# Score products in both halves of the partitions, two passes issued together, and the bias in 64-row products

## The chip, the core and the metric

The kernel runs on one core of a Trainium2 chip. The metric is the device time of one execution in microseconds. The core has five engines that run side by side: TensorE (PE, with its weight loads shown as PEld), VectorE (DVE), ScalarE (ACT), GpSimd (POOL) and SyncE (SP), which here only issues DMAs and waits. Engines meet through semaphores: an instruction waits until a count is reached, and adds to a count when it is done. Each engine takes its own instructions in order.

## What is computed

One transformer layer on 4 sequences of 1024 tokens with 128 channels: a layer norm, attention with 16 heads of 8 channels and relative positions, and a mixture of 64 experts with a shared one. Attention is what the change touches. With `rp` the distance key - query, clipped to -31..31:

```
q, k, v = heads of xn @ w_qkv.T          # q scaled by 8 ** -0.5
attn = q k^T
     + (q @ rpe_k_table)[.., rp]         # by query and distance
     + (k * scale @ rpe_q_table)[.., rp] # by key and distance
attn = softmax(attn)
out  = attn v + (sums of attn by distance) @ rpe_v_table
x    = x + out @ w_proj.T + b_proj + experts(xn) + shared(xn)
```

There are 4 x 16 = 64 pairs of sequence and head, called heads below. Scores of one head are 1024 x 1024.

## The kernel before

**Score rows.** Float32 factors are cut into bfloat16 parts. One score tile has 32 keys (partitions of the output) and up to 512 queries (columns), and is one product whose contraction runs over rows 0 to 72 or 0 to 78 of `Ks` (keys) and `Qs` (queries): 48 rows of six combinations of parts of q and k (`q_stack`, `k_stack`), three rows for the negated row maximum (`ROW_M`, filled by `Qs<-mparts`), and rows for the constant bias of far distances (`q_far`, `k_far`; 6 more rows for the keys above the window). Four such tiles, one for each 32 partitions of the output, fill a bank of PSUM: this is a *unit* of 128 keys `J` and one half of the queries. A head has 16 units. Near the diagonal (96 columns for each 32 keys) the bias depends on the exact distance; it is added by products with `eye3` (a stack of three 32 x 32 identities) as weights and a window `WT` of three parts (96 rows) as the moving side.

**Two passes.** Pass 1 makes the scores of a head; DVE takes maxima out of PSUM (L1408, one instruction a unit). Then DVE forms the row maximum, PE turns it (L914), DVE cuts it in three parts (`mparts`, L1421 to L1425) and SP writes them to the three rows `ROW_M` of `Qs` (L488). Pass 2 makes the same scores again, now less the maximum, and ACT takes their exponentials to `PT` (L1096). PE multiplies them with the values (`values`, products `PS<-PT,Vst`) and sums them by distance (`near`, products `PS<-WP,TOE`).

**The order of the work** is written out by hand. Every engine runs `iteration(i, c, peeled)` for head `h`, on PE, DVE and ACT in 16 slots `s`. In slot `s`, PE makes unit `s` of pass 1 of head `h + 1` and unit `s - 6` of pass 2 of head `h` (in slots 0 to 5 the last units of head `h - 1`). Each pass has two banks of PSUM of its own, so a unit waits until the one before last has been read (`s1_read` by DVE, `s2_read` by ACT).

**The window's round trip.** The near bias is prepared ahead, and goes through memory twice to be shifted by distance. In slot 11 PE makes the query part of head `h + 4` (L918, `PS<-Qs,tab`); ACT copies it to `dq_e` (L1115); SP writes it to `dq_d` (L544) and reads it back sheared as `dq_s` (L483). In slot 5 of the next iteration PE transposes `dq_s` and adds the key part (L944 and `PS<-tab,Ks`); ACT, DVE and POOL cut it in parts `ajp`; SP writes these to `aj_d` (L524) and reads them, sheared again, as the windows `WT` (L498).

**SP's queue.** In each iteration SP goes through one list in order: `TOE` (every second head), `dq_s` (waits until `dq_d` has landed), the three maximum rows (wait for `mparts`), four loads for the queries of head `h + 4` (`load_queries`), three windows of head `h + 2` (L498), three loads of keys of head `h + 4` (`load_keys`), `aj_d` of head `h + 3` (waits for POOL), `dq_d` of head `h + 4` (waits for ACT's copy). Some iterations have others between: `acc_d` and `xn_d` in the first eleven, weights of experts in iterations 13, 16, 22 and 24.

The 16 steps of the experts' products run alone after head 29, between 762 us and 846 us of the trace, and the loop over heads then goes on.

**Padding.** Lines 975 to 977 add instructions on PE that do nothing else than raise `paced`, so that each head has 1024 instructions on PE (`BLOCK`, `PER_HEAD`).

## Time and profile before

| | |
|---|---|
| median of 3 runs | 1529.62 us (1525.92 to 1534.31) |
| span of the profiled execution, first to last instruction | 1522.0 us |
| busy: PE, DVE, ACT, POOL | 87%, 73%, 52%, 36% of the span |
| score products (`PS<-Qs,Ks`) | 11904, 666.4 us busy |
| bias products (`PS<-WT,eye`) | 4352, 294.7 us busy |
| maxima by DVE (L1408) | 1024, 689.7 us busy, 699 ns each |
| packets moved by SP's DMA queue | 155414, 52.5% of the 16 DMA engines' span |
| mean granted clock of TensorE | 0.937 |

The page gives no time for the profiled execution apart from its span; the span is 7.6 us under the median of the runs. Busy times of PE are those of overlapping instructions whose ends are modelled: four products in four column groups run at once, so PE's busy share says little about how much of it is taken. DMA-issuing instructions are not counted as busy on any engine; they are seen in the timeline as SPq.

### The profile page before, as it was taken

To read this page: it belongs to the slowest core of one execution; us is meant where nothing else is said; L and a number is where in the kernel's file an instruction comes from. 1 tells how busy PE (TensorE), PEld (TensorE's weight loads), DVE (VectorE), ACT (ScalarE), POOL (GpSimd) and SP (SyncE) were. 2 spreads that over 40 slices of the span, in tenths; PEclk is the share of its full clock that TensorE was granted. 3 is DMA by queue.
4 is the path that set the end of the run, shared out by engine and by line. 5 is a ranking of instruction groups with operands and counts; after the bars stand their busy time and mean duration, and the time that the engine had idled before them with its cause. 6 is when DMAs were issued, how large, how long until landed. Compare 5 with 4: busy or idle time off the path is not lost. (4 is left out here: it accounts for less than half of the span.)

```text
span 1522.0 us, 75140 instructions
## 1 busy us (share of the span) xinstructions
PE 1325.6 (87%) x32698; PEld 895.9 (59%) x32698; DVE 1111.2 (73%) x2461; ACT 797.9 (52%) x1408; POOL 541.3 (36%) x552
## 2 busy tenths in 40 slices
PE   2785399999999999988989899999999999999887
PEld 1352256666666666655668565666666666666555
DVE  7684378888888888887764676777777767777762
ACT  1332135655665666655541455665666555656544
POOL 3453212222222222222434244444444444444423
PEclk9897559999999999999995799999999999999999
DMA  4444546666556555554564566666666666666532
GB/s 97 138 142 138 159 158 200 200 207 193 186 183 191 190 176 183 181 184 153 174 189 145 160 183 182 183 192 198 186 183 196 183 176 180 190 183 183 149 104 58
DMA packets 167209, 260.10 MB, mean 171 GB/s; under 512 B 33980, under 2 KB 89397, under 8 KB 166886
## 3 DMA queue, kind: packets, MB, share of 16 engines
q1 hardware_dynamic: 155414, 248.46, 52.5%
q0 software_dynamic: 11472, 6.83, 3.7%
q8 instruction: 264, 4.33, 1.1%
q14 instruction: 59, 0.48, 0.1%
HBM read 145.14 MB, written 112.37 MB: 169 GB/s over the span
## 5 line engine op out<-in xcount | busy, mean ns | idle before, releaser
L1408 DVE TRANSPOSE_TENSOR_REDUCE tops<-PS 128x16 f32<-128x512 f32 x1024 | 689.7, 699 | 190.1 <-PE PS L697 183.9
L1096 ACT ACTIVATE PT<-PS 128x512 f32<-128x512 f32 x1024 | 590.2, 596 | 423.4 <-PE PS L697 416.1
L697 PE MATMUL PS<-Qs,Ks 73*32 73x512 bf16 (+29 forms) x11904 | 666.4, 322 | 66.8 <-DVE tops L1408 45.6
L697 PEld LDWEIGHTS PS<-Qs,Ks 73*32 73x32 bf16 (+1 forms) x11904 | 308.9, 97 | 266.7 <-DVE tops L1408 94.0
L697 PE MATMUL PS<-PT,Vst 128*9 128x256 f32 (+7 forms) x7552 | 345.4, 286 | 12.6 <-issue 12.1
L638 POOL COPY WP<-PT 128x768 f32<-128x768 f32 x128 | 105.3, 822 | 645.4 <-ACT PT L1096 460.9
L697 PE MATMUL PS<-WT,eye 96*32 96x96 bf16 (+2 forms) x4352 | 294.7, 206 | 0.2 <-issue 0.2
L697 PEld LDWEIGHTS PS<-PT,Vst 128*9 128x9 f32 x7552 | 187.8, 91 | 82.6 <-issue 32.3
L697 PEld LDWEIGHTS PS<-WT,eye 96*32 96x32 bf16 x4352 | 186.8, 99 | 22.5 <-issue 1.2
L657 POOL TENSOR_TENSOR ajp<-dq_s,ajp 128x508 bf16<-128x508 f32 x128 | 147.3, 1151 | 10.4
L626 POOL DMA_INDIRECT acc_d<-XNA,tok_i x64 | 100.8, 1575 | 78.8 <-DMA acc_d<-XNA,tok_i 66.2
L1120 ACT ACTIVATE ajp<-PS 128x508 bf16<-128x508 f32 x128 | 76.8, 600 | 95.4 <-PE PS L697 95.4
L655 POOL CAST ajp<-dq_s 128x508 bf16<-128x508 f32 x128 | 78.7, 615 | 125.2 <-DVE dq_s L1449 125.2
L944 PE MATMUL PS<-ident,dq_s 127*128 127x127 f32 x512 | 86.5, 295 | 39.5 <-DMA dq_s<-dq_d 39.3
L697 PE MATMUL PS<-WP,TOE 128*32 128x32 f32 x6144 | 110.1, 197 | 5.4 <-issue 4.7
L697 PEld LDWEIGHTS PS<-WP,TOE 128*32 128x32 f32 x6144 | 103.8, 111 | 18.3 <-issue 17.4
L1449 DVE TENSOR_TENSOR dq_s<-PS,ajp 128x508 f32<-128x508 f32 x128 | 83.2, 650 | 27.9 <-ACT ajp L1120 27.9
L1115 ACT ACTIVATE dq_e<-PS 128x1024 f32<-128x1024 f32 x64 | 65.6, 1024 | 41.7 <-PE PS L697 41.7
L944 PEld LDWEIGHTS PS<-ident,dq_s 127*128 127x128 f32 x512 | 58.4, 151 | 46.9 <-issue 44.2
L1454 DVE TENSOR_TENSOR Ym<-PS,ymask 128x256 f32<-128x256 f32 x64 | 27.2, 425 | 75.6 <-PE PS L697 75.6
L697 PE MATMUL PS<-PT,WT 128*88 128x512 f32 (+2 forms) x128 | 56.0, 632 | 18.5 <-DVE Ym L1290 6.2
L697 PE MATMUL PS<-tab,Ks 79*128 79x127 bf16 x512 | 53.6, 231 | 0.0
(199 smaller groups left out, 1025.9 us busy)
## 6 DMA issues: line engine op xcount, KB each, us to landing
aj_d<-ajp SPq DMA_DIRECT2D x64, 768.0 KB
WT<-aj_d SPq DMA_DIRECT2D x192, 256.0 KB
dq_d<-dq_e SPq DMA_DIRECT2D x64, 512.0 KB, 5.3
dq_s<-dq_d SPq DMA_DIRECT2D x64, 512.0 KB, 3.9
TOE<-toe_d SPq DMA_DIRECT2D x33, 768.0 KB, 5.8
q_stack<-PT SPq DMA_DIRECT2D x24, 256.0 KB, 2.5
Qs<-q_stack SPq DMA_DIRECT2D x64, 96.0 KB
Ks<-k_stack SPq DMA_DIRECT2D x64, 96.0 KB
```

What stands on the lines that cost most here:

```text
L626: pool.indirect_dma_start(out=acc_d, out_offset=bass.IndirectOffsetOnAxis(ap=tok_i[:, 1 + half, n:n + 1], axis=0), in_=Y[:, n, :], in_offs ...
L638: pool.tensor_copy(WP[:, 4 * part:4 * part + 4, :], src).then_inc(win_in[part], 1)
L655: pool.tensor_copy(low[:, 0], r1).then_inc(aj_mid, 1)
L657: pool.tensor_tensor(low[:, 1], r1, low[:, 0], ALU.subtract).then_inc(aj_parts, 1)
L697: return pe.matmul(o, l, r, start=start, stop=stop, skip_group_check=True)
L944: pe.matmul(PS[:, bank, a * P:a * P + DIST], dq_s[0:DIST, J * P:(J + 1) * P], ident[0:DIST, 0:DIST], start=a == 0, stop=False, is_transpos ...
L1096: act.activation(PT[:, TILE + N * J + 512 * half:TILE + N * J + 512 * half + 512], PS[:, 2 + u % 2, :], ACT.Exp).then_inc(s2_read, 1)
L1115: act.activation(dq_e[:, :], MISC, ACT.Copy).then_inc(dq_copied, 1)
L1120: act.activation(ajp[:, 0, 4 * part:4 * part + 4, 0:DIST], PS[:, 6 + part, :].rearrange("p (a n) -> p a n", n=P)[:, :, 0:DIST], ACT.Copy). ...
L1408: dve.tensor_reduce(tops[:, (h + 1) % 2, s // 2, 16 * (s % 2):16 * (s % 2) + 16], PS[:, s % 2, :].rearrange("p (c i) -> p c i", i=TILE), A ...
L1449: dve.tensor_tensor(dst, src, ajp[:, 0, 4 * part:4 * part + 4, 0:DIST], ALU.subtract).then_inc(aj_copied, 1)
L1454: dve.tensor_tensor(Ym[:, :].rearrange("p (t a x) -> p a t x", t=NJ, x=4), PS[:, 6, 0:256].rearrange("p (a t x) -> p a t x", t=NJ, x=4), y ...
```

## The change

1. `Qs`, `Ks` and `tab` get 128 partitions. The 48 + 15 = 63 rows of the contraction (`ROW_M` moves from 64 to 48) lie in partitions 0 to 62 and again in 64 to 126. Queries are written to both halves. Keys are written once: even key tiles `J` to the upper half, odd ones to the lower. `tab` has three planes, the last one for odd tiles in the lower half.
2. A score product of tile `J` takes its rows from half `J % 2`, so it uses 64 rows. Pass 1's unit and pass 2's unit of one slot have key tiles three apart, so they are in different halves.
3. The new `units` waits for everything that either unit needs, and then issues their products in turn: the first pieces of both, the second pieces of both, the bias of both; the two counts `s1_ready` and `s2_ready` are raised at the end.
4. The bias of a window is two 64-row products: `eye3` over the first two parts, and `eye64` over the third part, which lies in planes 4 and 5 of `WT`, 32 rows for each pair of `s`.
5. DMAs follow: maxima six times instead of three, queries nine instead of four, windows eight instead of three (shorter runs of 512 instead of 1024 elements), keys six instead of three.
6. Keys are projected in the column order that suits this; `near` goes round the four column groups evenly; the padding of PE's instructions (L975 to L977) is dropped; DVE makes `eye64` once.

The diff, cut to its core:

```diff
-ROW_M = 64
-ROW_L = 73
-ROW_K = 73
-ROWS = 79
+ROW_M = 48
+ROW_L = 57
+ROW_K = 57
+ROWS = 63
+HALF = 64
...
-        QUERIES = 16 * 4
-        KEYS = 16 * 3
+        QUERIES = 16 * 9
+        KEYS = 16 * 6
+        WINDOWS = 16 * 8
+        MAXIMA = 16 * 6
...
             def load_queries(h):
-                sp.dma_start(Qs[0:48, r, :], q_stack[...]).then_inc(stack_in[r], 16)
-                sp.dma_start(tab[0:48, r, :, :], tab_stack[...]).then_inc(stack_in[r], 16)
-                sp.dma_start(Qs[ROW_M:ROW_M + 3, r, :], zero_d).then_inc(stack_in[r], 16)
-                sp.dma_start(Qs[ROW_M + 6:ROW_M + 12, r, :], q_far[hh, :, tok]).then_inc(stack_in[r], 16)
+                for side in range(2):
+                    top_row = HALF * side
+                    sp.dma_start(Qs[top_row:top_row + 48, r, :], q_stack[...]).then_inc(stack_in[r], 16)
+                    sp.dma_start(Qs[top_row + ROW_M:top_row + ROW_M + 3, r, :], zero_d).then_inc(stack_in[r], 16)
+                    sp.dma_start(Qs[top_row + ROW_M + 6:top_row + ROW_M + 12, r, :], q_far[hh, :, tok]).then_inc(stack_in[r], 16)
+                for v, row, m in ((0, 0, 0), (1, 0, 1), (1, HALF, 2)):
+                    sp.dma_start(tab[row:row + 48, r, m, :], tab_stack[...]).then_inc(stack_in[r], 16)
...
+            def load_windows(t):
+                for side in range(2):
+                    for row, planes, part, s in ((0, (0, 4), 0, 0), (TILE, (0, 4), 1, 0), (0, (4, 6), 2, 0), (TILE, (4, 6), 2, 2)):
+                        row += HALF * side
+                        sp.dma_start(WTb[row:row + TILE, t % 3, planes[0]:planes[1], :, :].rearrange("p s j n -> p s (j n)"),
+                                     shear(t % 2, part, side, s, planes[1] - planes[0])).then_inc(wt_in[t % 3], 16)
...
-                    for n in range(3):
-                        sp.dma_start(Qs[ROW_M + n:ROW_M + n + 1, ...], mparts[:, n, :]).then_inc(mrow_in, 16)
+                    for side in range(2):
+                        for n in range(3):
+                            row = HALF * side + ROW_M + n
+                            sp.dma_start(Qs[row:row + 1, ...], mparts[:, n, :]).then_inc(mrow_in, 16)
...
+            def scores(h, bank, J, half, n):
+                ins, row, r = None, HALF * (J % 2), h % RING
+                for s, k, w in pieces(J, half)[n]:
+                    key = P * (J // 2) + TILE * s
+                    ins = mm(PS[TILE * s:TILE * s + TILE, bank, w[0] - 512 * half:w[1] - 512 * half],
+                             Ks[row:row + k, r, key:key + TILE], Qs[row:row + k, r, w[0]:w[1]], start=n == 0)
+                return ins
+
+            def bias(h, bank, J, half, low):
+                ins, row = None, HALF * (J % 2)
+                for s, w, a in near_columns(J, half):
+                    eye = eye64[row:row + HALF, TILE * (s // 2):TILE * (s // 2) + TILE] if low else eye3[row:row + HALF, :]
+                    ins = mm(PS[TILE * s:TILE * s + TILE, bank, w[0] - 512 * half:w[1] - 512 * half], eye,
+                             WTb[row:row + HALF, h % 3, 4 + s % 2 if low else s, J // 2, a:a + w[1] - w[0]], start=False)
+                return ins
+
+            def units(first, second):
+                if first is not None:
...
+                    wait(pe, s1_read, SLOTS * h + u - 1)
+                if second is not None:
+                    h, u = second
+                    if u == 0:
+                        pe.wait_ge(mrow_in, MAXIMA * (h + 1))
+                    wait(pe, s2_read, SLOTS * h + u - 1)
...
+                for n in range(2):
+                    for k, *unit in both:
+                        last[k] = scores(*unit, n) or last.get(k)
+                for low in range(2):
+                    for k, *unit in both:
+                        last[k] = bias(*unit, low) or last[k]
...
-                    if on(1):
-                        unit(i, c + 1, s, 0)
+                    behind = (h, s - LAG) if s >= LAG else (h - 1, s + SLOTS - LAG)
+                    units((h + 1, s) if on(1) else None, behind if 0 <= behind[0] < HEADS else None)
...
-                    if s >= 12 and h >= 0:
-                        spare = BLOCK - PER_HEAD - (EXTRA if j_r == 2 else EXTRA + 1 if h == LISTS else 0)
-                        pause(spare // 4 + (s - 12 < spare % 4))
```

**How instructions move.** The first place is SP's list in a middle iteration, from the maximum rows to the last load for the queries. Before:

```order
L488 DMA Qs<-mparts 1x32x32 [waits mparts_ready]
L488 DMA Qs<-mparts 1x32x32 x2
L452 DMA Qs<-q_stack 48x1024 [waits s2_ready]
L453 DMA tab<-tab_stack 48x256
L455 DMA Qs<-zero_d 3x1024
L456 DMA Qs<-q_far 6x1024
```

The same place in the changed kernel:

```order
L506 DMA Qs<-mparts 1x32x32 [waits mparts_ready]
L506 DMA Qs<-mparts 1x32x32 x5
L454 DMA Qs<-q_stack 48x1024 [waits s2_ready]
L456 DMA Qs<-zero_d 3x1024
L457 DMA Qs<-q_far 6x1024
L454 DMA Qs<-q_stack 48x1024
L456 DMA Qs<-zero_d 3x1024
L457 DMA Qs<-q_far 6x1024
L459 DMA tab<-tab_stack 48x128 x3
```

Seven DMAs have become 15, with the same waits at the same two of them.

The second place is the rest of SP's list, from the windows to `dq_d`. Before:

```order
L498 DMA WT<-aj_d 32x4x1024 [waits s2_ready,aj_out]
L498 DMA WT<-aj_d 32x4x1024 x2
L461 DMA Ks<-k_stack 48x1024
L463 DMA Ks<-k_far 3x1024 x2
L524 DMA aj_d<-ajp 128x3x1024 [waits wt_in0,aj_parts]
L544 DMA dq_d<-dq_e 128x1024 [waits dq_in,dq_copied]
```

And in the changed kernel:

```order
L485 DMA WT<-aj_d 32x4x512 [waits s2_ready,aj_out]
L485 DMA WT<-aj_d 32x4x512
L485 DMA WT<-aj_d 32x2x512 x2
L485 DMA WT<-aj_d 32x4x512 x2
L485 DMA WT<-aj_d 32x2x512 x2
L468 DMA Ks<-k_stack 48x2x256
L471 DMA Ks<-k_far 3x2x256 x2
L468 DMA Ks<-k_stack 48x2x256
L471 DMA Ks<-k_far 3x2x256 x2
L540 DMA aj_d<-ajp 128x3x1024 [waits wt_in0,aj_parts]
L560 DMA dq_d<-dq_e 128x1024 [waits dq_in,dq_copied]
```

Six DMAs have become 14 before `aj_d`, which with `dq_d` stays at the end of the list.

The third place is PE's stream in slot 6, where pass 2 of a head begins (`Qs,Ks` are score products, `WT,eye` bias products; "32x512" is 32 keys by 512 queries). Before:

```order
L697 MATMUL PS<-Qs,Ks 32x352 [waits s1_read]
L697 MATMUL PS<-Qs,Ks 32x384
L697 MATMUL PS<-Qs,Ks 32x416
L697 MATMUL PS<-Qs,Ks 32x448
L697 MATMUL PS<-Qs,Ks 32x160
L697 MATMUL PS<-Qs,Ks 32x128
L697 MATMUL PS<-Qs,Ks 32x96
L697 MATMUL PS<-Qs,Ks 32x64
L697 MATMUL PS<-WT,eye 32x96 x3
L697 MATMUL PS<-WT,eye 32x64
L697 MATMUL PS<-Qs,Ks 32x512 [waits s2_read,mrow_in]
```

In the changed kernel:

```order
L713 MATMUL PS<-Qs,Ks 32x352 [waits s2_read,mrow_in,s1_read]
L713 MATMUL PS<-Qs,Ks 32x384
L713 MATMUL PS<-Qs,Ks 32x416
L713 MATMUL PS<-Qs,Ks 32x448
L713 MATMUL PS<-Qs,Ks 32x512 x2
L713 MATMUL PS<-Qs,Ks 32x32
L713 MATMUL PS<-Qs,Ks 32x64
L713 MATMUL PS<-Qs,Ks 32x160
L713 MATMUL PS<-Qs,Ks 32x128
L713 MATMUL PS<-Qs,Ks 32x96
L713 MATMUL PS<-Qs,Ks 32x64
```

The wait for the maximum rows (`mrow_in`) stood behind pass 1's unit 6 and now stands ahead of it, and the products of the two units alternate.

## Rows read from the trace of the kernel before

**Rows 1.** Two stretches: length, busy PE, PEld, DVE, ACT, POOL, clock, DMA share, GB/s
```profile
420.00:690.00 270.00, 246.27 (x6960) 166.41 (x6958) 230.69 (x521) 161.43 (x286) 71.63 (x84) 1.00 0.59 184
862.00:1440.00 578.00, 538.52 (x15125) 369.28 (x15121) 427.67 (x880) 344.92 (x605) 252.44 (x245) 0.99 0.65 184
```
**Rows 2.** L1404 on DVE, once a head, 190:780 and 840:1490: count, durations, first and last start
```profile
L1404 DVE TENSOR_REDUCE top<-tops x30: 587/597/623, 198.4 to 762.6; 128x32 f32<-128x256 f32 x30
L1404 DVE TENSOR_REDUCE top<-tops x34: 580/612/622, 846.6 to 1480.6; 128x32 f32<-128x256 f32 x34
```
**Rows 3.** Chain that ended last, 862:1440, shares by line
```profile
by line: PE PS L697 47.3%; DMA dq_d<-dq_e 12.6%; DMA dq_s<-dq_d 9.7%; DVE tops L1408 8.5%; PE PS L944 5.5%; issue 4.7%; ACT dq_e L1115 3.4%; DVE dq_s L1449 3.0%; PE PS L932 2.0%; ACT PT L1096 1.9%; PE PS L914 0.5%; DVE mparts L1421 0.2%; DV
```
**Rows 4.** SP's timeline, one iteration: start, us from first issue to last end, count
```profile
546.80 0.33 SPq L483 DMA_DIRECT2D dq_s<-dq_d  x1
549.92 1.78 SPq L488 DMA_DIRECT2D Qs<-mparts  x3
551.88 0.44 SPq L452 DMA_DIRECT2D Qs<-q_stack  x1
552.36 0.42 SPq L453 DMA_DIRECT2D tab<-tab_stack  x1
552.83 0.30 SPq L455 DMA_DIRECT2D Qs<-zero_d  x1
553.17 0.27 SPq L456 DMA_DIRECT2D Qs<-q_far  x1
553.54 1.86 SPq L498 DMA_DIRECT2D WT<-aj_d  x3
555.45 0.43 SPq L461 DMA_DIRECT2D Ks<-k_stack  x1
555.92 0.61 SPq L463 DMA_DIRECT2D Ks<-k_far  x2
559.32 0.39 SPq L524 DMA_DIRECT2D aj_d<-ajp  x1
560.22 1.34 SPq L544 DMA_DIRECT2D dq_d<-dq_e  x1
...
565.03 0.32 SPq L483 DMA_DIRECT2D dq_s<-dq_d  x1
```
**Rows 5.** SP's waits, 862:1440: us in total, times, longest
```profile
SPq L524 <- POOL ajp L657: 87.0, 31, 6.8
SPq L488 <- DVE mparts L1425: 63.4, 30, 4.7
```
**Rows 6.** DMA issues: dq_d 420:690 and 862:1440, maxima 420:690, median us to landing
```profile
dq_d<-dq_e SPq DMA_DIRECT2D x14, 512.0 KB, 4.8
dq_d<-dq_e SPq DMA_DIRECT2D x30, 512.0 KB, 5.7
Qs<-mparts SPq DMA_DIRECT2D x42, 2.0 KB, 1.7
```
**Rows 7.** L544 (dq_d), 862:1440: landing, shortest, median, longest
```profile
DMA to landing us min/median/max: 4.9/5.7/6.8
```
**Rows 8.** Issues of windows (420:690) and maxima (862:1440): ns min/median/max
```profile
L498 SPq DMA_DIRECT2D WT<-aj_d x42: 320/428/1412, 420.4 to 670.9; - x42
L488 SPq DMA_DIRECT2D Qs<-mparts x90: 518/588/1713, 873.8 to 1428.4; - x90
```
**Rows 9.** PE's timeline near slot 5: start, us, count
```profile
550.84 0.94 PE L697 MATMUL PS<-Qs,Ks 79*32 79x512 bf16 x16
551.61 0.21 PE L697 MATMUL PS<-WT,eye 96*32 96x96 bf16 x4
551.76 0.65 PE L944 MATMUL PS<-ident,dq_s 127*128 127x127 f32 x4
```
**Rows 10.** DVE's last cut of the maxima, and ACT's first exponential of that head
```profile
549.72 0.17 DVE L1425 CAST mparts<-mx 32x32 bf16<-32x32 f32 x1
554.44 1.08 ACT L1096 ACTIVATE PT<-PS 128x512 f32<-128x512 f32 x2 [0.19 <-PE PS L697]
```

More of the change, by code:

```diff
@@ L496, in iteration @@
                     wait(sp, s2_ready, SLOTS * h)
[L497 to L499 removed]
+                    load_windows(t)
                 if on(4):
@@ L813, in scores @@
-                return bias(bank, half, J, r3) or ins
-            def unit(i, c, u, which):
-                h, r = c, c % RING
-                ready, read, bank = ((s1_ready, s1_read, 0), (s2_ready, s2_read, 2))[which]
-                if which == 0 and u == 0:
-                    pe.wait_ge(stack_in[r], QUERIES * (h // RING + 1))
-                    pe.wait_ge(keys_in[r], KEYS * (h // RING + 1))
-                    pe.wait_ge(wt_in[h % 3], 48 * (h // 3 + 1))
-                if which == 1 and u == 0:
-                    pe.wait_ge(mrow_in, 48 * (h + 1))
-                wait(pe, read, SLOTS * h + u - 1)
-                J, half = u // 2, u % 2
-                scores(bank + u % 2, half, J, r, h % 3).then_inc(ready, 1)
+                            own[n].append((s, ROWS if kind == "U" else ROW_L, w))
@@ new lines, in pieces, with near_columns @@
+                            n += 1
+                return own
+            def near_columns(J, half):
+                own = []
+                for s in range(4):
+                    t = 4 * J + s
+                    w = span(max(TILE * (t - 1), 0), min(TILE * (t + 2), N), half)
+                    if w:
+                        own.append((s, w, w[0] - TILE * (t - 1)))
+                return own
+            def scores(h, bank, J, half, n):
[5 more added lines that the diff above has]
+                return ins
```

117 lines of the change are left out of this document (52 added, 65 removed).

## The prediction, written before the changed kernel ran

> **What bounds the kernel now.** I read first which stretches repeat: L1404 runs once a head, and its starts give the period, (762.6 - 198.4) / 29 = 19.46 us a head before the experts' stretch and (1480.6 - 846.6) / 33 = 19.21 us after it [rows 2]. These 62 periods are 1198 of the 1522 us, and the change touches little else. Then the busy times: DVE, which has no overlap inside it, is busy 230.69 / 270 x 19.46 = 16.6 us a head in the first stretch (where it also routes tokens) and 427.67 / 578 x 19.21 = 14.2 us in the second [rows 1]. So no engine but PE can be full, and PE's busy time is of overlapping products. Third the chain: in the second stretch 22.3% of it are the transfers of `dq_d` and `dq_s`, most of the rest is PE [rows 3]. That is the round trip, ACT's copy, `dq_d`, `dq_s`, PE's slot 5, then six slots of PE, and again: the two transfers are 0.223 x 19.21 = 4.3 us a head on average over heads that hang on them and heads that don't.
>
> Last, and it decides here, SP's own timeline [rows 4]. One iteration takes 18.23 us from one `dq_s` to the next (546.80 to 565.03). SP goes idle in it three times: 3.1 us for the maxima, 2.8 us for POOL's `ajp` (556.53 to 559.32), and for the landing of `dq_d`, issued at 560.22, 4.81 us before the next `dq_s`. The rest is issuing, back to back: each DMA holds SP for 0.27 to 0.6 us plus some 0.05 us to the next.
>
> **SP's cycle without its two idle waits.** From the starts in [rows 4]: `dq_s` 0.37 (with its gap), three maxima 1.83, `q_stack` 0.48, `tab` 0.47, `zero_d` 0.34, `q_far` 0.37, three windows 1.91, `k_stack` 0.47, two `k_far` 0.66, `aj_d` about 0.45, and `dq_d` to the next `dq_s` 4.81. Sum 12.2 us, so in 18.2 us SP has 6.0 us of slack. In the second stretch the waits for POOL and for the maxima are (87.0 + 63.4) / 31 = 4.9 us a head [rows 5]; that is what SP can give there before it sets the pace.
>
> **The changed list, part by part**, at the same price for the same kind of DMA [rows 4]; whether a half-sized DMA costs SP less is bounded below.
> - Maxima: six at 0.61 = 3.66 us (was 1.83).
> - Queries: (0.48 + 0.34 + 0.34) twice and `tab` three times 0.47 = 3.73 us (was 1.66).
> - Windows: eight. Three took 1.91 us in this iteration with one of them held up; the median is 0.428 [rows 8], 0.47 with its gap, so eight are 3.76 us, and 4.4 us with one held up by 0.6 (1.91 less three times 0.47 is 0.5, and the longest issue of all is 1.41).
> - Keys: twice 0.47 and four times 0.33 = 2.26 us (was 1.13).
> - `dq_s` 0.37, `aj_d` 0.45, `dq_d` until landing and next `dq_s` 4.81.
>
> Sum 3.66 + 3.73 + 4.4 + 2.26 + 0.37 + 0.45 + 4.81 = 19.7 us. This is a loop by itself: `dq_s` waits for `dq_d` of the iteration before, and `dq_d` stands at the end of the list. Nothing that PE gains shortens it. SP's waits for `mparts`, `s2_ready`, `aj_parts` and `dq_copied` should be over when it arrives: `aj_d` now comes some 14 us after `dq_s`, where POOL's parts were ready after 12.5 us (546.80 to 559.32).
>
> First stretch: 19.7, and weights of experts (8 DMAs), `acc_d` and `xn_d` (about 22) stand in the same list, some 20 us in all by 0.43 to 1 us each (an estimate from `k_stack` at 0.43 and `dq_d` at 1.34), 0.7 us a head: 20.4 us against 19.46, +0.9 x 29 = +27 us. Second stretch: `dq_d` lands after 5.7 instead of 4.8 us [rows 6], and one maximum in four is held up (median 0.588, longest 1.713) [rows 8], say 0.5 us a head: 19.7 + 0.9 + 0.5 = 21.1 us against 19.21, +1.9 x 33 = +63 us.
>
> **What is hidden.** PE: 16 products of three units take 0.77 us to the next (550.84 to 551.61), 0.26 a unit, 32 units 8.2 us a head; if two halves run side by side that is 4.1 us less. Bias: four products cost at most 0.15 us (551.61 to 551.76) [rows 9], and the 4352 of them are 17 such groups a head, which double: at most +2.6 us, below it near zero where they fall beside the other half. Both lie under SP's cycle. Dropped padding: nothing in the trace shows it as cost or gain; I take 0, within -0.2 and +0.5 us a head, as PE has slack now. Shorter `WT` runs, 768 instead of 384 packets, and 96 KB more for queries: the DMA engines are 59 and 65% busy [rows 1], 11.5 and 12.5 us of a period; twice the queries is +96 KB on about 3.6 MB moved in a head, and more packets than bytes at most +15%, 1.8 us on engines with 7 us to spare. It can lengthen `dq_d`'s landing, which is in the range. Start: memsets, `eye64` and six maxima for the first head, +2 us, inside the rounding.
>
> A place where the chip's notes speak: the Trainium skill, "DMA: Bandwidth & Descriptors", Rules for kernel authors, says that two transfers to disjoint partition halves are no gain since they serialize on the same engines, and to use one of 128 partitions. Here both halves are loaded apart, with the same bytes twice. The trace bears it out on the issuing side, where every DMA holds SP whatever its size (0.30 us for `zero_d`, 6 KB, and 0.44 for `q_stack`, 96 KB) [rows 4]. By that rule too the sum goes up; it changes no term.
>
> Sum: 1522.0 + 27 + 63 = 1612 us of span, + 7.6 by which the median stands over the span: I predict **1620 us**.
>
> **Bounds.** Low: nothing held up and each DMA at its median (19.0 us), landing 4.9 at best in the second stretch [rows 7], other DMAs 10 us in all. That is 19.4 and 19.1 us a head, -5 us in all: 1525. Half-sized windows at the shortest issue seen (0.320) [rows 8] take another 0.9 us: 1470. High: landing 6.8 [rows 7] and every group held up once more: 21.3 and 22.8 us a head, +53 and +119: 1702.
>
> **Rivals.**
> 1. *SP's issues overlap or shrink and the engines gain.* If the 16 more DMAs held SP less than 6.0 us in the first and 4.9 us in the second stretch, that is 0.3 to 0.37 us each, SP stays off the path. Then the round trip binds, with six slots of PE in it, 12 units, of which half go: -1.5 us a head; DVE's 16.6 allows that. 62 x -1.5 = -93: 1437 us. For it: the engines' waits name PE everywhere. Against it: only `zero_d`, `q_far` and `k_far` are near 0.3 [rows 4]. Chance 0.16.
> 2. *The maxima land late and PE holds pass 1 behind them.* From DVE's last cut (549.72 + 0.17) to the first exponential are 4.55 us [rows 10]; issues take 1.78 and landing 1.7 after the last issue begins [rows 4, 6], so about 1 us is spare. Six issues take 1.83 more: the exponential comes 0.8 to 1 us later, and since pass 1's unit 6 now waits too, DVE runs out. Where SP's cycle is not longer, the period is 19.3 + 0.9 less what PE gains elsewhere, 0 to 1 us: 19.2 to 20.2, that is 1525 to 1585 us. It would be told from mine by PE's wait for `Qs<-mparts` with SP idle. Chance 0.08.
> 3. *The halves don't run side by side.* PE then keeps its 8.2 us, gets 2.6 us of bias, and loses more at changes of shape. It had little slack, so 19.3 + 2.6 and more: 22 to 23 us, +200 us: 1730. Chance 0.05. The Trainium skill, "TensorEngine Tiling (Array Packing)", Key Properties, says that a change of tiling mode drains TensorE. Values keep 128 rows and alternate with the 64-row units, so by the rule there are some 16 drains more a head. At a change of that kind now (551.61 to 551.76, from 32-column tiles to a whole-array transpose) the row leaves at most 0.15 us for products and drain together [rows 9], 2.4 us a head, which SP's cycle covers unless this rival holds.
>
> **How the numbers follow.** Mine 0.68, the rivals 0.16, 0.08 and 0.05, 0.03 for what I haven't thought of. About 0.5% (8 us) either way is what a measurement can tell from none. Of my 0.68, bounds leave 0.03 within that and 0.03 below. Rival 1 is faster, rival 2 slower by two thirds, rival 3 slower. So faster 0.19, same 0.06, slower 0.75. The range leaves rivals 1 and 3 out and takes in mine: 1505 to 1700.
>
> **What would show it.** The starts of L1404 20 to 21 us apart. SP's timeline without idle time between `dq_s` and `aj_d`: about 13.5 us of issues end to end, and its waits for POOL's `ajp` and `mparts` near zero; only the wait for `dq_d` stays. PE's waits for `dq_s<-dq_d` in slot 5 up from few to nearly every head, and DVE's and ACT's idle time up with them. Two units together in 0.3 us or less if the halves run side by side. I am wrong if SP still idles 2 us or more for POOL or `mparts`, or if one of its DMAs takes clearly under 0.3 us.

## The result, and the profile after

The changed kernel takes 1830.83 us (median of 4 runs, 1815.33 to 1837.52) against 1527.77 us of the kernel before on the same chip: ratio 1.199, 95% interval 1.1915 to 1.2064. The prediction had the direction and missed the size: 1620 was forecast, with a range up to 1700.

Some executions of a kernel took longer at a lower granted clock, and differences, ratios and the table below leave them out: without them the medians of `b_mrow6`, `b_rest`, `b_shift`, `a_mrow3` and `a_shift` are 1778, 1608, 1691, 1760 and 1846 us, where the medians of all their runs are 1794, 1614, 1715, 1764 and 1849, and the profile of `b_shift` is of such an execution, at 1742.

The page of the changed kernel: span, busy PE and granted clock in 40 slices, queues, and the groups that answer to [rows 1, 5, 9].

```profile
span 1831.2 us, 84602 instructions
PE 1302.5 (71%) x36988; PEld 852.9 (47%) x37050; DVE 1111.4 (61%) x2462; ACT 796.6 (43%) x1408; POOL 540.8 (30%) x552
PE   3782776767667777777779677777776777777677
...
PEclk9895689898888888889875888888888889999888
...
q1 hardware_dynamic: 219542, 257.17, 45.1%
...
q8 instruction: 297, 4.87, 1.1%
...
PE 19%; SPq 8%; issue 7%; DMA 6%; DVE 6%; ACT 0%
...
L713 PE MATMUL PS<-Qs,Ks 57*32 57x512 bf16 (+29 forms) x11904 | 460.4, 347 | 235.4 <-issue 117.8
...
L713 PE MATMUL PS<-WT,eye 64*32 64x96 bf16 (+2 forms) x8704 | 288.8, 212 | 45.1 <-issue 45.0
```

Nobody became busier, everybody waits more. Score products are busy 460.4 us where they were 666.4, yet PE sat idle 235.4 us in front of them (66.8 before), half of it behind "issue", which means that nothing the profile shows held it. The clock's slices are 8 where nearly all were 9. SP's queue, 0% of the chain on the page of before, has 8% of it.

The two stretches (columns as in [rows 1]), the once-a-head DVE instruction as in [rows 2], and the chain of 1100:1700:

```profile
500.00:900.00 400.00, 291.38 (x9133) 188.50 (x9135) 266.05 (x606) 186.28 (x328) 87.20 (x102) 0.86 0.47 147
1100.00:1700.00 600.00, 435.19 (x14213) 287.65 (x14238) 358.92 (x738) 287.81 (x506) 206.72 (x200) 0.90 0.53 154
```
```profile
L1433 DVE TENSOR_REDUCE top<-tops x29: 582/599/636, 199.8 to 887.2; 128x32 f32<-128x256 f32 x29
...
L1433 DVE TENSOR_REDUCE top<-tops x31: 580/598/616, 1071.2 to 1786.2; 128x32 f32<-128x256 f32 x31
```
```profile
by line: PE PS L713 31.6%; issue 15.5%; DMA dq_d<-dq_e 8.4%; DVE tops L1437 7.1%; SPq L485 6.4%; DMA dq_s<-dq_d 5.8%; SPq L506 5.0%; PE PS L976 4.0%; DVE dq_s L1478 2.9%; SPq L459 2.3%; SPq L468 2.0%; SPq L471 1.8%; SPq L454 1.2%; PE PS L96
```

The period is (887.2 - 199.8) / 28 = 24.55 us a head, then (1786.2 - 1071.2) / 30 = 23.8 us, where it was 19.46 and 19.21 [rows 2]; 62 periods of some 4.8 us more are the 300 us. In the chain "issue" has 15.5%, 3.7 us a head, three times its share in [rows 3].

SP's timeline, the iteration that answers to [rows 4]; then its waits and PE's in 1100:1600 (total, times, longest), as in [rows 5]:

```profile
612.28 0.32 SPq L499 DMA_DIRECT2D dq_s<-dq_d  x1
613.60 3.79 SPq L506 DMA_DIRECT2D Qs<-mparts  x6
617.44 0.58 SPq L454 DMA_DIRECT2D Qs<-q_stack  x1
...
619.71 1.23 SPq L459 DMA_DIRECT2D tab<-tab_stack  x3
621.04 3.68 SPq L485 DMA_DIRECT2D WT<-aj_d  x8
...
627.85 0.39 SPq L540 DMA_DIRECT2D aj_d<-ajp  x1
628.34 0.43 SPq L560 DMA_DIRECT2D dq_d<-dq_e  x1
633.25 0.33 SPq L499 DMA_DIRECT2D dq_s<-dq_d  x1
640.50 0.52 SPq L506 DMA_DIRECT2D Qs<-mparts  x1
```
```profile
SPq L499 <- DMA dq_d<-dq_e: 90.8, 21, 7.6
SPq L506 <- DVE mparts L1454: 41.6, 17, 6.9
```
```profile
PE PS L713 <- issue: 89.7, 67, 4.8
PE PS L713 <- DVE tops L1437: 29.1, 43, 0.8
PE PS L976 <- DMA dq_s<-dq_d: 10.0, 7, 2.4
```

The issue costs came out as priced: six maxima 3.79 us, eight windows 3.68. POOL's `ajp` is no longer waited for. But after its next `dq_s` SP waits 6.9 us for the maxima (633.58 to 640.50): it is not SP alone that sets the pace, PE is late too: it stood still 89.7 us of 500 with "issue" as the reason, 4.8 us at the longest. The first stretch lost more than the second: its periods are 4.15 us over the 20.4 forecast, the second's 2.7 us over 21.1.

### The profile page after: what moved, and what is told of

The parts are those of the page before. It is cut to its first block and busy times, and to the rows that moved or that the text cites. A ratio compares the mean times of both kernels' runs of the same rounds, so it can differ in the third digit from the quotient of the medians.

```text
span 1831.2 us, 84602 instructions
## 1 busy us (share of the span) xinstructions
PE 1302.5 (71%) x36988; PEld 852.9 (47%) x37050; DVE 1111.4 (61%) x2462; ACT 796.6 (43%) x1408; POOL 540.8 (30%) x552
## 3 DMA queue, kind: packets, MB, share of 16 engines
q8 instruction: 297, 4.87, 1.1%
## 5 line engine op out<-in xcount | busy, mean ns | idle before, releaser
L713 PE MATMUL PS<-Qs,Ks 57*32 57x512 bf16 (+29 forms) x11904 | 460.4, 347 | 235.4 <-issue 117.8
L713 PE MATMUL PS<-PT,Vst 128*9 128x256 f32 (+7 forms) x7552 | 379.4, 312 | 56.4 <-issue 55.2
L713 PEld LDWEIGHTS PS<-Qs,Ks 57*32 57x32 bf16 (+1 forms) x11904 | 169.8, 93 | 434.9 <-issue 216.8
L713 PE MATMUL PS<-WT,eye 64*32 64x96 bf16 (+2 forms) x8704 | 288.8, 212 | 45.1 <-issue 45.0
L713 PEld LDWEIGHTS PS<-WT,eye 64*32 64x32 bf16 x8704 | 260.3, 102 | 87.9 <-issue 56.5
L713 PEld LDWEIGHTS PS<-PT,Vst 128*9 128x9 f32 x7552 | 171.6, 96 | 171.8 <-issue 85.2
L976 PE MATMUL PS<-ident,dq_s 127*128 127x127 f32 x512 | 108.5, 350 | 68.5 <-DMA dq_s<-dq_d 68.3
L673 POOL TENSOR_TENSOR ajp<-dq_s,ajp 128x508 bf16<-128x508 f32 x128 | 147.7, 1154 | 10.4
L713 PE MATMUL PS<-WP,TOE 128*32 128x32 f32 x6144 | 88.8, 199 | 19.1 <-issue 17.9
L713 PEld LDWEIGHTS PS<-WP,TOE 128*32 128x32 f32 x6144 | 79.3, 112 | 26.9 <-issue 22.2
L1143 ACT ACTIVATE dq_e<-PS 128x1024 f32<-128x1024 f32 x64 | 65.6, 1024 | 49.3 <-PE PS L713 49.3
L713 PE MATMUL PS<-tab,Ks 128*128 128x127 bf16 x512 | 65.3, 266 | 0.0
```

The lines of the kernel that those rows point to most:

```text
L673: pool.tensor_tensor(low[:, 1], r1, low[:, 0], ALU.subtract).then_inc(aj_parts, 1)
L713: return pe.matmul(o, l, r, start=start, stop=stop, skip_group_check=True)
L976: pe.matmul(PS[:, bank, a * P:a * P + DIST], dq_s[0:DIST, J * P:(J + 1) * P], ident[0:DIST, 0:DIST], start=a == 0, stop=False, is_transpos ...
L1143: act.activation(dq_e[:, :], MISC, ACT.Copy).then_inc(dq_copied, 1)
```

## What stops TensorE with nothing to wait for

I numbered PE's instructions in the trace and looked where it stopped without a semaphore. The stops stand at multiples of 256: in `b_shift`, 53 of 57 successive stops of 0.5 us and more lie a whole number of 256 instructions apart. The queue named instruction (q8) brings such blocks: 297 packets of 16 KB, 4.87 MB, for some 76200 instructions of PE in the changed kernel (297.6 times 256), and 264 packets for 67700 in the kernel before (264.6 times 256). An example from the run `b_shift` below, PE's timeline:

```profile
1038.93 0.37 PE L697 MATMUL PS<-PT,Vst 128*9 128x96 f32 x6
1040.73 0.60 PE L697 MATMUL PS<-PT,Vst 128*9 128x64 f32 x10 [1.42 <-issue]
```

PE stops in the middle of 16 value products. The packet with the next block ran from 1038.33 to 1039.28, and PE went on 1.44 us after its end; over all stops of 0.5 us and more at block ends in the changed kernel this lag is 1.28 to 1.52 us (10th to 90th percentile, median 1.39). The packet began only 1.0 us before PE was through (1039.30), so whether a block end costs anything depends on what PE does around it: where PE waits for another engine anyway, the block arrives unseen (0.06 us a block in `b_mrow6`, below).

The kernel before has 1024 instructions a head, four blocks, so its block ends stand at the same four places in every head, and the empty instructions are what keeps them there. The changed kernel has 1157 and no padding: 4.5 blocks, whose ends move through all places. This and two more quantities, worked out from the traces: stops over 0.3 us at block ends, their sum over the number of blocks in 420:690 and 862:1440; time at the lower clock, 1.2 GHz, for each period of the loop over heads, from 240 us on and without the experts' part; last maximum landed after DVE's last cut, median in 862:1440. In the slower kernels the experts' part lies later and so within 862:1440 (887 to 982 us in `b_mrow6`); without it the stops come out nearly the same.

```
kernel        median   instr.  stop per  low clock  maxima landed
               us      a head  block us  us a head   us
before        1524-39  1024     0.14        0.4       3.7
b_actq        1523     1024     0.15        0.4       3.5
b_nopad       1617     1007     0.41        2.6       3.8
b_rest        1608     1024     0.28        1.6       3.7
b_bias2       1631     1143     0.46        1.7       3.6
b_shift       1691     1024     0.53        6.1       3.0
b_mrow6       1778     1024     0.06        7.8       6.2
b_splist      1828     1024     0.14        8.8       6.3
a_both        1557     1024     0.51        1.6       3.0
h_wide_m3     1621     1024     0.47        1.3       3.0
a_thin        1699     1157     0.74        2.9       3.6
h_wide        1761     1024     0.36        5.0       5.8
h_wide_p64    1790     1024     0.46        5.7       5.5
h_wide_p192   1802     1024     0.60        4.8       5.4
a_mrow3       1760     1157     0.71        3.8       4.1
a_nolow       1776     1024     0.43        5.5       5.9
h_wide_p128   1894     1024     0.83        8.2       5.2
a_actq        1816     1157     0.81        5.5       5.7
after         1831     1157     0.90        5.7       5.8
a_shift       1846     1157     0.85        6.0       5.9
```

Kernels with one time only (`a_both`, `a_thin`, `a_nolow`, `b_splist`) had the kernel before at 1538 beside them; the others were run four to ten times, with the kernel before at 1524 to 1539. Where DMAs of a head are counted below, `dq_s` is left out: 15 before, 31 in the changed kernel.

## The experiments

**First round: SP's list or TensorE.** Theory A: SP's longer list and the stops at block ends, each a part. Theory B: the list is all. Theory C: the products' shapes.

`a_thin`: the changed kernel with SP's list cut to 15 DMAs a head; after the first round of buffers the loads for the odd tiles' half and the maxima for it are left out, so its output is another one.

```diff
-                for side in range(2):
+                for side in range(2 if h < RING else 1):        # queries, keys; maxima and windows alike
```

> The changed kernel, with the DMAs for the lower half of the partitions left out after the first round of buffers (so SP's list has 15 DMAs a head again, not 31; the scores of odd key tiles are computed from stale rows). Theory A (two causes: SP's list costs about 1 to 1.5 us a head over the old period, and PE's stalls at every 256th instruction, where the next block of instructions is fetched, cost the rest): SP's share goes, PE's stalls stay: 1620 to 1720 us, L1433 21 to 22.5 us apart, PE still stalled some 2 to 4 us a head at block boundaries. Theory B (SP's list is all of it; PE's stalls only fill time that SP leaves): 1440 to 1540 us.

Measured 1699.04 us, beside 1538 of the kernel before: some 140 us of the 300 are gone with the list, not all. B falls.

`a_nolow`: the changed kernel without the second of the two 64-row bias products, and with three empty instructions a head, 1024 in all (bias of every third window left out).

```diff
-                for low in range(2):
+                for low in range(1):
...
+                    if s == 12 and h >= 0:
+                        pause(3)
```

> The changed kernel without the products with eye64 (the third part of the near bias is left out), and 3 empty instructions a head on PE, so that a head has 1024 instructions on PE again (four blocks of 256) instead of 1157. SP's list stays at 31 DMAs. Theory A: stalls at block boundaries fall to under 1 us a head, the period becomes SP's cycle of about 20.5 us: 1600 to 1680 us. Theory B: SP's list is untouched, so at most the 2.6 us a head of bias products could go, and none of it is on SP's path: 1780 to 1840 us. Theory C (64-row products next to 128-row ones make PE wait at each change of shape): changes of shape are the same, so 1780 us or more.

Measured 1775.82 us. Only some 60 us, a miss: a whole number of blocks is not yet a good place for their ends, and the maxima still came late.

`a_both`, both edits together:

> Both edits at once: no eye64 products and 1024 instructions a head on PE, and SP's list of 15 DMAs. Theory A: neither cause is left, and what the halves side by side give is seen: 17.3 to 18.5 us a head, 1420 to 1500 us. Theory B: the same as with the thin list alone, within 1%. Theory C: over 1600 us, since the changes of shape are all there.

Measured 1556.73 us. So with a short list, three maxima, the third part of the bias left out and 1024 instructions, scores in both halves cost 19 us against 1538 and gain nothing at this place of the block ends. C, which wanted over 1600, falls; A had hoped for a gain that isn't there. Whether it would be there at another place was not tested: PE stopped 0.51 us a block here for 0.14, 1.5 us a head more.

`b_splist`: the kernel before, with the same bytes in the changed kernel's 31 DMAs a head (queries 9, keys 6, windows 8, maxima 6, each cut in smaller ones). Of its edit, the part on the maxima:

```diff
-                    for n in range(3):
-                        sp.dma_start(Qs[ROW_M + n:ROW_M + n + 1, h % RING, :]..., mparts[:, n, :])
+                    for n in range(3):
+                        for z in range(2):
+                            sp.dma_start(Qs[ROW_M + n:ROW_M + n + 1, h % RING, 512 * z:512 * z + 512]..., mparts[16 * z:16 * z + 16, n, :])
```

> The kernel before, with the same bytes in 31 DMAs a head on SP instead of 15 (each cut in two or three, the numbers by kind as in the changed kernel). PE's instructions and their padding are untouched. Theory A: SP's cycle of 20 to 21 us sets the period: 1590 to 1660 us, SP's waits for POOL's parts and for the maxima near zero, stalls of PE at block boundaries as before. Theory B: 1780 us or more.

Measured 1828.46 us, with the old products and hardly a stop at a block end. In this single run the list alone makes the old kernel as slow as the changed one: A's 1590 to 1660 is a miss. B had this right, and `a_thin` and `a_both` wrong. Something in the list costs far more than its length.

**Second round: which DMAs, and is it the number of instructions.** All on the kernel before.

`b_mrow6` has only the edit just shown (three DMAs more); `b_rest` all the others (13 more, maxima in three).

> The kernel before with only the row maxima copied in six DMAs of half the size in place of three, the count of the changed kernel. Theory M (what SP's longer list costs is mostly that the maxima land later and pass 1 waits behind them): 2.1 us a head more before they have landed, twice if the lower clock follows, so 1660 to 1800 us. Rival L (the whole list's length costs, by SP's cycle): 3 DMAs more of 16 that SP's slack of 5 to 6 us takes in: 1530 to 1560 us.

> The kernel before with every other DMA of a head cut as in the list with 31 DMAs (queries 9, keys 6, windows 8), the maxima left in three. Theory M: the maxima leave SP at once, so most of the 290 us that the full list cost are gone: 1560 to 1640 us. Rival L: 13 DMAs more, 5.5 us a head, nearly all of the list's price: 1740 to 1820 us.

Measured 1794.06 us and 1614.08 us (ratio 1.042, 1.036 to 1.048). Three DMAs of 0.6 us cost 240 us, thirteen others 70. Theory M holds. The waits of PE in `b_mrow6`, 862:1440, then what follows such a wait (columns as in [rows 1]):

```profile
PE PS L698 <- DMA Qs<-mparts: 42.1, 21, 2.5
...
PE PS L698 <- issue: 4.8, 7, 1.7
```
```profile
862.00:1440.00 578.00, 513.42 (x11391) 348.02 (x11381) 348.52 (x721) 266.38 (x476) 205.13 (x200) 0.82 0.54 153
```
```profile
1006.00:1018.00 12.00, 11.62 (x346) 8.45 (x340) 8.26 (x19) 6.41 (x13) 2.40 (x2) 0.96 0.47 143
1018.00:1020.40 2.40, 0.41 (x26) 0.25 (x14) 1.29 (x2) 0.53 (x2) 1.35 (x2) 1.00 0.07 6
1020.40:1024.40 4.00, 4.00 (x68) 2.48 (x69) 2.29 (x4) 1.81 (x4) 2.81 (x4) 0.57 0.67 171
1024.40:1028.20 3.80, 3.67 (x86) 1.98 (x86) 2.83 (x6) 2.62 (x5) 1.78 (x2) 1.00 1.07 305
```

PE waits 2.0 us in 21 of 22 heads. After the wait (0.41 us busy of 2.4) the granted clock falls to 0.57 on average for 4 us, that is nearly all at 1.2 GHz, and PE does 68 products in 4.0 us, 17 a us, where it did 346 in 12, 29 a us.

The mean clock of 0.82 can't be turned into a price for a head, because this stretch takes in the experts' part, and the clock is low there in the kernel before too (52 us, all else of its trace after 250 us 30). A stretch of that kind, then one behind a wait for the maxima, then the heads behind the experts' part:

```profile
914.80:1007.00 92.20, 87.09 (x779) 67.17 (x782) 42.16 (x106) 24.00 (x51) 28.91 (x29) 0.50 0.48 138
1303.90:1314.10 10.20, 10.20 (x203) 6.00 (x191) 4.74 (x9) 4.50 (x7) 3.34 (x3) 0.50 0.76 218
1007.00:1440.00 433.00, 380.57 (x9595) 251.57 (x9587) 276.26 (x556) 217.67 (x383) 160.56 (x154) 0.89 0.56 158
```

The price is seen when the periods of the loop, from the starts of the once-a-head DVE instruction after 240 us, are sorted by the time at the lower clock in them:

```
kernel     periods, mean us, without low clock     with 8.5 to 12 us of it     with more
before     54, 18.9                                none                        1, 23.6
b_mrow6    16, 20.5                                28, 24.2                    11, 26.1
b_splist    6, 20.6                                29, 24.4                    13, 26.0
```

So the wait of 2.0 us by itself makes a head 1.6 us longer (20.5 for 18.9), and the lower clock behind it another 3.7 to 5.6 where it comes. The period of `b_mrow6` is 23.8 us before the experts' part and 23.0 behind it, for 19.45 and 19.2: 4.1 us a head, which over 62 periods are the 250 us that this execution (1789) lost. Its larger part, 2.5 us, is the clock. All 42 stretches of low clock outside the experts' part begin within 2 us of a pause of PE of 1.2 us or more, and 28 of them last 10.2 us; of the 61 such pauses 19 had none behind them. In `b_splist` it is 53 of 53.

`b_nopad` drops the empty instructions and nothing else; `b_bias2` drops them and issues each bias product twice (so its bias counts twice).

```diff
-                    if s >= 12 and h >= 0:
-                        spare = BLOCK - PER_HEAD - (EXTRA if j_r == 2 else EXTRA + 1 if h == LISTS else 0)
-                        pause(spare // 4 + (s - 12 < spare % 4))
```

> The kernel before without its empty instructions in TensorE's rounds 12 to 15: 1007 instructions a head where there were 1024, nothing else. Theory F (TensorE's instructions arrive in blocks of 256 and it stops at a block's end until the next has landed; the 17 empty ones keep the four block ends of a head at the same, idle places): the ends now drift through the dense rounds, the stop per block grows from 0.18 us towards 0.4, so 1545 to 1590 us. Rival S (TensorE has slack and fewer instructions cost nothing): 1520 to 1535 us.

> The kernel before without the empty instructions and with every bias product issued twice (the bias is counted twice, so its output is another one): 68 more matrix products with their weights a head, 1143 instructions where the changed kernel has 1157; DMA list, tile shapes and order are those of before. Theory F: stops at block ends as in the changed kernel (0.9 us a block, 4.5 blocks a head, less what idle time hides): 1620 to 1750 us. Rival S: about 3 us of products a head, in slack: 1525 to 1570 us.

Measured 1617.22 us (ratio 1.051, 1.043 to 1.058) and 1631.37 us (1.060, 1.054 to 1.067). Dropping 17 instructions a head costs 80 us, more than F said; adding 136 to that costs only 14 more, in F's range. So it is not the number.

**Third round: the place of the block ends, and the maxima on two queues.**

`b_shift`: the kernel before with 96 more empty instructions once, at the start.

```diff
-START = 58
+START = 58 + 96
```

> The kernel before with 96 more empty instructions at TensorE's start (154 for 58) and nothing else: every block of 256 instructions now ends 96 instructions earlier in each head's work, four times a head at the same places as each other. Theory F (what dropping the empty instructions costs is where the blocks end, not how many instructions there are): 1560 to 1640 us, the first kernel's 1538 being the well placed case. Rival N (only the number of instructions a head matters): 1530 to 1550 us.

Measured 1715.37 us (ratio 1.111, 1.101 to 1.120), above even F's range. PE's waits in 862:1440, of the kernel before and of `b_shift` (whose experts' part ends at 922 us), and a piece of the chain of the latter:

```profile
PE PS L697 <- issue: 10.9, 20, 1.9
```
```profile
PE PS L697 <- issue: 40.7, 36, 2.2
```
```profile
1034.39 0.86 PE PS L697 x36
1035.66 3.64 PE PS L697 x111
1039.30 1.42 issue
...
1042.74 0.68 DVE tops L1408
...
1045.84 3.10 DMA Qs<-mparts
```

In this piece the stop comes out of PE's dense rounds, just ahead of the head's last maxima, and moves them; the transfer of `Qs<-mparts` that follows is on the chain here, but in only 6 heads of the whole run (2 in the kernel before), and it lands no later after the cut. The loss is the stops and the clock behind them: 26 periods without low clock take 19.9 us for 18.9, and the clock is low 6.1 us a head for 0.4. The same instructions, 1024 a head, 96 places on: 1691 us for 1524, 167 us.

`a_actq`: the changed kernel with the upper half's three maxima issued by ScalarE in its slot 4; `b_actq`: the kernel before with its third maximum there.

```diff
+                    if s == 4 and on(0):
+                        act.wait_ge(mparts_ready, h + 1)
+                        for n in range(3):
+                            act.dma_start(Qs[HALF + ROW_M + n:HALF + ROW_M + n + 1, h % RING, :]..., mparts[:, n, :]).then_inc(mrow_in, 16)
```

> The changed kernel with the three copies of the maxima for the upper half issued by ScalarE (round 4), beside SyncE's three for the lower: the same DMAs, on two queues. Theory M (late maxima are the largest part of the loss): they leave in some 2 us where it took 4.2, the waits and the low clock behind them shrink, 1640 to 1740 us, the rest being the block ends and the list. Rival L (the list's length as such): SyncE is 2.1 us shorter a head with 28 DMAs left: 1740 to 1790 us. Rival C (the products' shapes): no change, 1810 to 1840 us.

> The kernel before with the third copy of the maxima issued by ScalarE (round 4) and two by SyncE. Theory M (pass 1's first product waits for the last of these copies, and has hardly any room before): they land about 0.6 us earlier, 1500 to 1540 us. Rival: ScalarE's wait and issue, 0.6 us and more in front of an exponential, come back on the path: 1545 to 1590 us.

Measured 1815.74 us and 1523.16 us (ratio 1.0004, 0.9972 to 1.0035). Neither moves. `a_actq` did not make the test it was meant for: the last of the six was issued 3.05 us after the cut instead of 4.45 (medians), but the last one landed 5.7 us after it, as in the changed kernel (5.8). So the issuing is not all of the delay; what held the landing is not known. `b_actq` lands 0.3 us earlier and gains nothing. It is the nearest to a better kernel in this study, and is equal to the one before.

`h_wide`: the scores' part alone. Scores in halves and units together as in the change, but the bias in 96-row products from three windows, as before; 26 DMAs and 1024 instructions a head.

```diff
-                    eye = eye64[row:row + HALF, TILE * (s // 2):TILE * (s // 2) + TILE] if low else eye3[row:row + HALF, :]
-                    ins = mm(PS[...], eye, WTb[row:row + HALF, h % 3, 4 + s % 2 if low else s, J // 2, a:a + w[1] - w[0]], start=False)
+                    ins = mm(PS[...], eye3[0:WIN, :], WTb[0:WIN, h % 3, s, 4 * (J % 2) + J // 2, a:a + w[1] - w[0]], start=False)
```

> The scores' part of the change alone: score rows in both halves and units issued together, but the bias in 96-row products from 96-row windows as before (3 window DMAs, 26 of a head in SyncE's list for 31), and 3 empty instructions a head so that there are 1024. Theory M: six copies of maxima as in the changed kernel, so still slow: 1700 to 1780 us. Rival L (length of the list): 5 DMAs shorter than the kernel without the low bias products (1776 us): 1660 to 1700 us.

Measured 1761.47 us (ratio 1.155, 1.149 to 1.161), in M's range.

**Fourth round: move the block ends, on purpose.** Three kernels as `h_wide` with START raised by 64, 128 and 192, and `a_shift`, the changed kernel with 96.

> The kernel with the scores' part of the change alone and 1024 instructions a head, with 64 more empty instructions at TensorE's start. Theory F (the place of the block ends decides): the four kernels of this row (0, 64, 128, 192) differ by over 80 us among each other, and the best of them is at 1600 to 1680 us. Rival G (shapes, maxima and list decide): all four within 30 us of 1761.

> The changed kernel with 96 more empty instructions at TensorE's start, the edit that cost the kernel before 190 us. It has 1157 instructions a head, so block ends pass through every place of the head in either case. Theory F: no change beyond 20 us, 1810 to 1850 us. Rival (the 96 instructions cost by something else, the start of the program or the number of instructions): 100 us and more on top, 1930 us.

Measured: `h_wide_p64` 1790.49, `h_wide_p128` 1894.35, `h_wide_p192` 1802.04 us; `a_shift` 1848.89 us (ratio 1.208, 1.201 to 1.215, overlapping the changed kernel's). The place makes 133 us between worst and best of four, and nothing measurable where the ends drift anyway: both as F said. But none of the four places saves `h_wide`: the best stays at 1761, not 1600 to 1680. In the worst, PE's waits in 862:1440 (experts' part included) are

```profile
PE PS L710 <- issue: 91.7, 51, 4.7
```

**Fifth round: the maxima in the changed kernel.** `a_mrow3` and `h_wide_m3` leave out the upper half's three copies of the maxima, so odd tiles' scores are computed without them.

```diff
-                    for side in range(2):
+                    for side in range(1):                       # the copies of mparts only
```

> The changed kernel without the three copies of the maxima into the upper half (the odd key tiles' scores are computed without them, so its output is another one): 28 DMAs a head in SyncE's list for 31, all else the same. Theory M (the maxima land 2.1 us later than before and pass 1 waits): a good part of the 300 us comes back, 1660 to 1750 us. Rival I (1157 instructions a head: stops at block ends in the dense rounds hold the pace whether or not the maxima are early): 1780 to 1830 us.

> The scores' part of the change alone with 1024 instructions a head, and without the copies of the maxima into the upper half (again another output): 23 DMAs a head. Theory M: 1580 to 1650 us, down from 1761. Rival I does not bear on it, since its block ends are the same as at 1761 us: there the length of the list and the shapes are left, 1700 to 1760 us.

Measured 1763.84 us (ratio 1.150, 1.140 to 1.159) and 1621.35 us (1.055, 1.047 to 1.062). In `h_wide` the three copies are worth some 150 us (ratio 1.155 to 1.055), as M said. In the changed kernel they are worth some 75 (1.199 to 1.150), and 1764 lies between M's range and the rival's. With 1157 instructions PE still stops 0.71 us a block there (0.90 with the copies, 0.47 in `h_wide_m3`); it is likely, but not shown, that part of what the maxima give back is lost again there.

## Why the prediction was wrong

**Where the time is.** By removing parts, as ratios to the kernel before beside each run: with scores in both halves, 8 DMAs more and other places of the block ends, 1.055 (some 84 us); with three more copies of maxima, 1.155 (another 150); with the 64-row bias, 5 DMAs and 133 instructions more, 1.199 (another 70). In the other order the bias comes first, 1.055 to 1.150 (145 us), and the maxima then cost 75: the two share a bill.

**SP's list, priced right.** The sum was 19.7 to 21.1 us. Measured in 1100:1700: maxima 4.2 (3.66 forecast), the rest of the list 11.2 (10.4), `dq_d` to `dq_s` 5.6 (4.8 and 5.7), `aj_d` with its two waits 0.6, `dq_s` 0.4: 22 us. SP held by each DMA for 0.27 to 0.6 us, and the missing wait for POOL, are right. Two readings were loose: SP idles 2.8 us for the maxima in [rows 4], not 3.1, which takes in the issue of `dq_s`; and its rows on how long SP is held do not bear out the rule on disjoint halves that it cites beside them, which speaks of the engines that move the data.

**The step that failed** is the sentence "SP's waits for `mparts`, s2_ready, aj_parts and dq_copied should be over when it arrives". For `mparts` it is false: 1.9 us a head remain (41.6 us in 500, above), because DVE's cut comes late, because PE does. In 420:900, where the forecast was 4.15 us too low, it is 47.4 us in 14 waits, 2.4 us a head. I took SP's cycle as a loop by itself. In fact it runs from the maxima through the list, `dq_d` and `dq_s` to PE's slot 5, and by PE's next 14 slots back to the maxima; whatever delays PE in it is added. Two things did.

**Rival 2 was the stronger one, and was mispriced.** I had late maxima as an alternative worth 0.9 us a head. The issues were right (1.83 us more; the last one ends 4.45 us after the cut for 2.32), and they landed 2.1 us later (5.8 for 3.7 us); PE held in `b_mrow6` 2.0 us a head, which made a head 1.6 us longer and not 0.9. What I left out was the clock, another 2.5 us a head there: 4.1 us in all. In the trace of before the clock stood at 1.00 and 0.99 [rows 1], which I read as a constant; it was a condition.

**Dropped padding, taken as 0 within -0.2 and +0.5 us a head, "as PE has slack now".** It is +80 us on the kernel before (1.3 us a head), and the place of the block ends alone +167. Nor did PE have slack: from the start of one product to the next, at full clock and with idle times over 0.15 us left out, the trace of before gives 19.4 us a head, about as much as its period (an estimate: the mean for each kind of neighbours times their number). Nothing in the grouped views of before shows this, but the idle time "issue" in front of products that wait for nothing, 10.9 us in the stretch, was its trace, and I did not ask where in the code those stops stood.

**What was right:** the halves do run side by side. PE's timeline at full clock:

```profile
1206.12 0.41 PE L713 MATMUL PS<-Qs,Ks 63*32 63x480 bf16 x13
1206.35 0.27 PE L713 MATMUL PS<-WT,eye 64*32 64x32 bf16 x10
...
1208.77 0.41 PE L713 MATMUL PS<-Qs,Ks 63*32 63x512 bf16 x12
1209.02 0.25 PE L713 MATMUL PS<-WT,eye 64*32 64x96 bf16 x7
1209.07 0.21 PE L713 MATMUL PS<-Qs,Ks 63*32 63x96 bf16 x1
```

A unit of each pass with its bias goes from 1208.77 to 1209.07, 0.30 us for two where the scores alone of one took 0.26 [rows 9]. By the estimate from starts of products, scores take 3.7 us of a head for 7.4. But it does not show in the end: `a_both`, with everything else taken away, is at 1557, with its stops at block ends at 0.51 us for 0.14. So rival 1's gain of the engines isn't seen either, with SP's list as short as before.

**Of rival 3 a part is left:** the halves run side by side, but the changes of shape cost. The Trainium skill, "TensorEngine Tiling (Array Packing)", Key Properties, says that a change of tiling mode drains TensorE, and the traces agree. From the start of the last value product (128 rows) to that of the next score product, medians at full clock in ns, by columns of that value product, and from the last bias product (96 columns) to the next value product (what stands further back is not the same in all, so the differences are estimates):

```
            rows of a score  128 col.  160  192  224  256   bias to value
before      73 or 79               45   91  246  181  196   36 (96 rows)
a_both      57 or 63              209  236  262  284  309  133 (64 rows)
h_wide_m3   57 or 63              209  229       283  309   43 (96 rows)
```

So a change into the 64-row mode takes 0.02 to 0.16 us more than the same neighbours take in one mode, and the way back 0.1; where the bias keeps 96 rows, as in `h_wide_m3`, the way back to the values costs nothing. There the price falls between scores and bias instead: 0.18 us for 0.07, 16 times a head, and 0.15 for 0.02 on the way back, 8 times. By the estimate of above the same value products take 4.8 us of a head for 3.8 in the changed kernel, the doubled bias 2.7 for 1.6, and all of PE's work 17.5 for 19.4; in `h_wide_m3` it is 18.5.

**PE's waits for `dq_s`** were to show in nearly every head; they are there in 7 of some 21. The round trip ends the chain in some heads, PE's stops in others.

**Left open.** The 84 us between the kernel before and `h_wide_m3` are not taken apart into list, order and places of block ends. Why the list's other 13 DMAs cost 70 us (`b_rest`) with SP's slack of 6 us was not tested; the stops at block ends doubled there (0.28 for 0.14), so they moved against the work. That the pauses make the clock fall rests on their order in time (42 of 42 and 53 of 53 stretches above), not on an experiment that changes one without the other; the kernels with most low clock are those with PE's waits or stops in dense rounds. The places of the block ends were moved in `h_wide`, the changed kernel and the kernel before alone, each at one to four places.

## What to carry to other kernels

Before costing an edit, look at the granted clock and at what keeps it: in a kernel at 0.99, a new pause of 2 us a head of the matrix engine cost 4 us, and more than half of that was the clock. When stretches of two kernels are compared, see that both hold the same work: the experts' part had moved into one of them here. Price a new wait by its effect on the clock as well as its length, and take a loop of waits through all engines, not one queue's list by itself. An edit that changes the number of TensorE's instructions in a periodic loop also moves the places where it waits for its next block: compare at several paddings before the edit is judged.

## What the runs showed of the hardware that was not expected

- TensorE's instructions come in packets of 16 KB, 256 at a time, and where it stops at a block's end it goes on 1.4 us after the packet with the next ones has ended. 96 empty instructions at the start, once, made 1524 us into 1691.
- Behind 42 of 61 pauses of PE, most of them 2 us long, the granted clock fell to 1.2 GHz, mostly for 10.2 us (`b_mrow6`). It was low 0.4 us a head in the kernel before and 8.8 in `b_splist`, whose products are the same.
- A change between products of 128 and of 64 rows took PE some 0.1 us, 0.16 at most, that the same neighbours in one mode did not.
- Three more DMAs on a critical hand-over (six of 1 KB for three of 2 KB) cost 240 us of 1538, thirteen others 70.
